# Causal mask of the softmax maxima: from a table added on VectorE to a bf16 product accumulated by TensorE

## The chip, the cores and the metric

The kernel runs on one core of a Trainium2 chip (trn2). The metric is the device time of one execution in microseconds (us), lower is better. Below, "before" is the kernel as it was and "after" the changed one.

## The reference, cut to what matters

The program computes four layers on x of shape (4, 1024, 128): an attention with a compressed key/value and rotary parts, a top-1 mixture of experts, a dilated attention, and a last mixture with gates. Only the first attention is touched:

```
q = concat(q_content, rope(q_rope))      # 16 heads, 8 + 32 per head
k = concat(k_content, rope(k_rope))
scores = einsum('bhqd,bhkd->bhqk', q, k) / sqrt(40)
scores = where(tril(ones(T, T)), scores, -inf)      # T = 1024
attn = softmax(scores, axis=-1)
out = einsum('bhqk,bhkd->bhqd', attn, v)
```

A softmax needs the maximum of each query's row over the keys up to itself. How this maximum comes about is what changes.

## The kernel before

**Units.** The 4 x 16 heads are worked as 32 units of two heads (`NU`). For each unit SyncE gathers queries and keys into the tiles `Qp` and `Kp` (four of each in rotation), with parts laid out so that one matmul over 120 rows gives the scores.

**Two passes.** A unit's scores are computed twice. The first pass (kind `mx`, L604) has queries on partitions and keys along the row: for query tile `qt` (0 to 7, each 128 queries) the keys 0 to 128(qt+1). VectorE takes the row maxima from it (L833 to L840). They are transposed (kind `mxT`, L608), negated (L847) and written by a DMA into row 120 of `Qp`. The second pass (kind `st`, L615) has keys on partitions; row 120 subtracts the maximum inside the product, ScalarE takes the exponential (L717), GpSimd zeroes what lies past the diagonal (L907), and TensorE multiplies by the values (kind `pv`, L632).

**Slots.** `S` is three PSUM tiles of 1024 columns, two banks of 512 each. Every `mx`, `st`, `rope`, `oT`, `mxT` and the like takes the next slot in rotation, and TensorE waits until what was in it has been drained. For the kinds of `BY_HALF` ("mx", "st", "rope") both the filling and the draining are signalled by half, with two steps of the semaphore for each item.

**The order** is written out beforehand in `Attn0.order`. Each of 12 steps of a unit issues one `st` and one `mx` (of a later unit, 12 + 3 steps ahead), every second step a `pv`; rotations of the next group of units and the next batch's preparation are strewn in between. All engines walk through the same list.

**The maxima.** An `mx` item is one query tile and one part of the keys: part 0 the first 512, part 1 the rest (for qt of 4 and more). Half h of the slot holds head h. A part 0 of a qt of 4 and more is a plain maximum into `first` (L833). Every other item ends on the diagonal: L836 adds the table `later` (zeros, then the 128x128 triangle `mqk` of 0 and -1e30) and takes the maximum in one fused instruction, followed by a read of the accumulator. After qt = 0 the two parts are merged (L840). That is 8 reduces, 16 fused instructions and one merge for each unit.

**Semaphores**: `made(kind)` counts what TensorE has filled, `done(kind)` what has been drained.

Of the kernel before, what the change touches and what calls it, by code (L numbers as in the profile page):

```python
# [7 lines left out]
F32R = mybir.dt.float32r  # L8
BF16 = mybir.dt.bfloat16
U32 = mybir.dt.uint32  # L10
ALU = mybir.AluOpType
ACT = mybir.ActivationFunctionType
AX = mybir.AxisListType
# [76 lines left out]
class Program:  # L90
# [44 lines left out]
    def sb(self, st, name, shape, dt=F32):  # L135
        return st.enter_context(self.nc.sbuf_tensor(name, shape, dt))
# [39 lines left out]

BY_HALF = ("mx", "st", "rope")


def free_half(p, lane, w, h):  # L180

    if w.before:
        kind, n = w.before
        lane.wait_ge(p.done(kind), 2 * n - 1 + h if kind in BY_HALF else n)
# [164 lines left out]
for n, (name, i) in enumerate((("cq", 0), ("cq", 1), ("ck", 0), ("ck", 1))):  # L349
    for later, kind in enumerate(("rope", "spin", "high", "low")):  # L350
        at = 8 + 4 * n + later
# [7 lines left out]
class Attn0:  # L359
    names = ("wkd", "wvd", "wo0")  # L360

    def __init__(self, p, st, route):
        self.route = route
        def sb(name, shape, dt=F32):
            return p.sb(st, name, shape, dt)
# [7 lines left out]
        self.cos, self.sin = within(p.low, 0, T), within(p.low, T, T)  # L373
        self.later = sb("later", [128, 512])
        self.xnT = within(p.mid, 0, T)
# [6 lines left out]
        self.P = [sb(f"P{i}", [128, 2, 512]) for i in range(NP0)]  # L382
        self.mx, self.first, self.mT = sb("mx", [128, 2, 8]), sb("first", [128, 2, 4]), sb("mT", [16, 128], F32R)
        self.oT, self.rec, self.osum = sb("oT", [128, 512]), sb("rec", [128, 4, 2]), sb("osum", [128, 4, 2, 9])
# [6 lines left out]
    def order(self, o):  # L391
        start = len(o.items)
# [9 lines left out]

        pieces = [(qt, part) for qt in range(7, -1, -1) for part in range(qt // 4 + 1)]

# [68 lines left out]
def shipped(p, lane, u, *names):  # L473

    for name in names:
        lane.wait_ge(p.sem(f"d_{name[1]}{u % 4}"), 128 * (u // 4 + 1))
# [21 lines left out]
def attn0_sync(p, k, f0, sp, ye):  # L498
    a = p.a
    x_in = a["x"].rearrange("(n p) d -> p n d", p=128)  # L500
    for i in range(2):
        ye.dma_start(p.x[:, 4 * i:4 * i + 4, :], x_in[:, 4 * i:4 * i + 4, :]).then_inc(p.sem("d_x").h, 16)
    for t, n in ((k.cos[:], "cos"), (k.sin[:], "sin"), (k.R["ck"][:], "wkr"), (k.later[:, 384:512], "mqk")):
        ye.dma_start(t, a[n]).then_inc(p.sem("d_c").h, 16)
# [35 lines left out]
CONSTS0, WEIGHTS0 = 16 * 4, 16 * 5  # L540


def attn0_tensor(p, k, pe, te):
    S, A, W = p.S, p.A, k.W
    for w in k.items:
        s = w.slot
# [12 lines left out]
        elif w.kind == "kv":  # L559
            pe.wait_ge(p.done("xnT"), w.n)  # L560
            pe.wait_ge(p.sem("d_w"), WEIGHTS0)
            for i in range(8):
                ins = te.matmul(S[s][:, 32 * i:32 * i + 32], k.xnT[:, 128 * i:128 * i + 128], k.wkv[:], start=True, stop=True)
# [4 lines left out]
        elif w.kind in ("cq", "ck"):  # L568
# [7 lines left out]
            for i in range(2):  # L576
                c = slice(512 * i, 512 * i + 512)
                ins = te.matmul(S[s][:, c], weight[:], src[:, c], start=True, stop=True)
# [18 lines left out]
        elif w.kind == "mx":  # L597
            u, qt, part = w.at
            Q, K, n = k.Q[u % 4], k.K[u % 4], min(512, 128 * (qt + 1) - 512 * part)
            pe.wait_ge(p.sem("g_ones"), 1)  # L600
            shipped(p, pe, u, "cq", "ck")
            for h in range(2):
                free_half(p, pe, w, h)
                te.matmul(S[s][:, 512 * h:512 * h + n], Q[0:120, h, 128 * qt:128 * qt + 128],  # L604
                          K[0:120, h, 512 * part:512 * part + n], start=True, stop=True).then_inc(p.made("mx").h, 1)
        elif w.kind == "mxT":
            pe.wait_ge(p.done("mx"), 24 * w.n)
            te.transpose(S[s][0:16, 0:128], k.mx[:].rearrange("p h n -> p (h n)"), p.ident[:]).then_inc(p.made("mxT").h, 1)  # L608
        elif w.kind == "st":
            u, qh, kb, c = w.at  # L610
# [122 lines left out]
def attn0_vector(p, k, f0, dve, ve):  # L733
    S, x = p.S, p.x
    ve.memset(k.later[:, 0:384], 0.0)
    for A in p.A:
        ve.memset(A[:], 0.0).then_inc(p.sem("v_zero").h, 1)
    for w in k.items:
        s = w.slot
# [21 lines left out]
        elif w.kind == "ln4":  # L761
            b = w.at[0]
            ln_apply(p, ve, k.xn, x[:, 8 * b:8 * b + 8, :], range(4, 8)).then_inc(p.sem("v_xn").h, 1)
            if b == 0:
                dve.wait_ge(p.sem("d_w"), WEIGHTS0)
                ve.tensor_scalar(k.W["wkd"][:], k.W["wkd"][:], k.gkv[:, 0:1], None, ALU.mult)
                ve.tensor_scalar(k.W["wvd"][:], k.W["wvd"][:], k.gkv[:, 0:1], None, ALU.mult).then_inc(p.sem("v_weights").h, 1)
# [57 lines left out]
        elif w.kind == "mx":  # L825
            u, qt, part = w.at
            if u:
                dve.wait_ge(p.made("mxT"), u)
            n = 128 * (qt + 1) - 512 * part
            for h in range(2):  # L830
                dve.wait_ge(p.made("mx"), 2 * w.n - 1 + h)
                if part == 0 and qt >= 4:
                    ve.tensor_reduce(k.first[:, h, qt - 4:qt - 3], S[s][:, 512 * h:512 * h + 512], AX.X, ALU.max).then_inc(p.done("mx").h, 1)  # L833
                    continue
                of = S[s][:, 512 * h:512 * h + n]
                ins = ve.tensor_tensor_reduce(out=of, in0=of, in1=k.later[:, 512 - n:512], scale=1.0, scalar=-3e38, op0=ALU.add, op1=ALU.max,  # L836
                                              accum_out=k.mx[:, h, qt:qt + 1])
                if qt == 0 and h == 1:
                    dve.then(ins)
                    ins = ve.tensor_tensor(k.mx[:, :, 4:8], k.mx[:, :, 4:8], k.first[:], ALU.max)  # L840
                ins.then_inc(p.done("mx").h, 1)
        elif w.kind == "mxT":
# [1648 lines left out]
```

## Time and profile before

| | |
|---|---|
| median of 3 runs | 1527.55 us (1525.64 to 1531.12) |
| profiled execution: span from its first to its last instruction | 1519.5 us |
| the runs' median above this span | 8.05 us |
| the first attention's units, from the first maxima to the last | 60 to 813 us of the span |
| TensorE busy in the span | 1254.7 us (83%) |
| VectorE busy in the span | 1153.3 us (76%) |

The profiled execution has no time of its own beside its span in the records. The 8.05 us are what lies around the span.

How to read the profile: PE is TensorE (PEld its weight loads), DVE VectorE, ACT ScalarE, POOL GpSimd, SP SyncE. "Busy" is the time covered by records of an engine. L604 is line 604 of the kernel. In `S<-Kp,Qp` the tile written stands ahead of the arrow and the tiles read behind it.

### The profile page before, as it was taken

Reading aid. Unit: us, or ns where it says so; the run is one execution under the profiler, and the core shown is the slowest. Engines: PE = TensorE matmul, PEld = TensorE weight load, DVE = VectorE, ACT = ScalarE, POOL = GpSimd, SP = SyncE. Lnnn points to the kernel's source line nnn. Section 1 sums busy time; section 2 is a strip of 40 time slices with the busy share of each in tenths; the row PEclk is TensorE's granted clock in tenths of the full one; section 3 lists DMA queues with packets and bytes.
Section 4 is the critical chain, followed back from the end, with each engine's and each line's share of the span. In section 5 each row is a group of like instructions: output and inputs, shape, how many; then the busy total and the mean of one; then the engine's idle time right before and its main releaser. Section 6 shows DMA issues by size and latency. Waiting matters only on the chain.

```text
span 1519.5 us, 38187 instructions
## 1 busy us (share of the span) xinstructions
PE 1254.7 (83%) x13524; PEld 854.0 (56%) x13524; DVE 1153.3 (76%) x3936; ACT 832.7 (55%) x2003; POOL 690.7 (45%) x1043
## 2 busy tenths in 40 slices
PE   5489899998899888999888899959988999557780
PEld 2344444445455454454444799947777778546660
DVE  5588787897898977989875755547799988755666
ACT  1145456554555544555556545438887767326663
POOL 3023232333233333324313454556687888674664
PEclk9689999998999989999999989977898877568995
DMA  4665726557266472573770221021111112222335
GB/s 112 102 104 83 117 36 94 90 84 117 32 89 113 62 120 36 84 127 47 122 221 28 83 59 37 22 65 45 45 46 47 54 51 75 94 73 79 89 87 172
DMA packets 73886, 123.25 MB, mean 81 GB/s; under 512 B 17534, under 2 KB 46083, under 8 KB 72800
## 3 DMA queue, kind: packets, MB, share of 16 engines
q1 hardware_dynamic: 63896, 104.97, 36.4%
q0 software_dynamic: 7616, 13.59, 2.8%
q10 hardware_dynamic: 2184, 2.25, 0.7%
q8 instruction: 108, 1.77, 0.5%
q14 instruction: 82, 0.67, 0.1%
HBM read 30.40 MB, written 17.60 MB: 32 GB/s over the span
## 4 chain that ended last, share of the span: by engine, by line
PE 39%; DVE 31%; issue 10%; POOL 8%; ACT 7%; DMA 4%; DVEq 1%; SPq 0%; ACTq 0%; POOLq 0%
DVE first L833 5%; PE A L632 5%; PE S L1099 5%; PE S L615 4%; PE S L604 4%; DVE S L836 4%; DMA Qp<-mT 2%; DVE tA L812 2%; POOL xq L1468 2%; PE A L1106 2%; PE S L1659 2%; DVE tB L813 2%; PE S L596 2%; PE S L194 2%; PE A L1670 2%
## 5 line engine op out<-in xcount | busy, mean ns | idle before, releaser
L717 ACT ACTIVATE P<-S 128x512 f32<-128x512 f32 (+3 forms) x768 | 333.4, 491 | 286.2 <-PE S L615 281.8
L907 POOL TENSOR_SCALAR_AFFINE_SELECT P<-P 128x256 f32<-128x256 f32 (+1 forms) x256 | 116.5, 459 | 390.2 <-ACT P L717 390.1
L615 PE MATMUL S<-Qp,Kp 121*128 121x512 f32 (+3 forms) x768 | 254.8, 396 | 35.1 <-DVE tB L813 9.6
L604 PE MATMUL S<-Kp,Qp 120*128 120x512 f32 (+3 forms) x768 | 255.0, 402 | 33.1 <-DMA Kp<-big 16.1
L836 DVE CUSTOM_DVE_ANT_0 S<-S,later 128x512 f32<-128x512 f32 (+3 forms) x512 | 239.0, 512 | 44.3 <-PE S L604 43.1
L604 PEld LDWEIGHTS S<-Kp,Qp 120*128 120x128 f32 x768 | 136.0, 199 | 168.0 <-issue 76.3
L615 PEld LDWEIGHTS S<-Qp,Kp 121*128 121x128 f32 x768 | 141.1, 195 | 111.4 <-issue 24.1
L833 DVE TENSOR_REDUCE first<-S 128x1 f32<-128x512 f32 x256 | 164.3, 683 | 48.8 <-PE S L604 48.6
L632 PE MATMUL A<-P,V 128*9 128x512 f32 (+3 forms) x1536 | 176.6, 508 | 5.1 <-POOL P L907 5.0
L2264 POOL DMA_INDIRECT yq<-yq,id x71 | 70.4, 991 | 51.5 <-DVE id L2221 23.2
L1896 POOL TENSOR_TENSOR prod<-mid,kT 128x128 f32<-128x128 f32 x160 | 68.2, 460 | 51.0 <-ACT mid L1727 34.4
L895 POOL TENSOR_TENSOR big<-tA,big 128x1024 fp32r<-128x1024 f32 x28 | 66.3, 2368 | 43.5 <-ACT big L679 43.5
L1767 ACT ACTIVATE low<-sc,mn 128x64 f32<-128x64 f32 x336 | 82.4, 336 | 4.8 <-DVE sc L1831 4.8
L1099 PE MATMUL S<-xgT,we 128*128 128x128 f32 x624 | 79.8, 283 | 2.9 <-ACT we L1122 2.2
L1099 PEld LDWEIGHTS S<-xgT,we 128*128 128x128 f32 x624 | 76.2, 199 | 3.5 <-issue 2.4
L1659 PE MATMUL S<-kT,Qm 32*32 32x64 f32 x4096 | 61.5, 231 | 19.1 <-issue 7.9
L1468 POOL DMA_INDIRECT xq<-n,posu x64 | 64.5, 1007 | 28.2 <-issue 13.6
L836 DVE DVE_READ_ACCUMULATOR2_ANT mx<- 128x1 f32 x512 | 71.1, 139 | 0.0
L1302 POOL DMA_INDIRECT ys<-yo,id x39 | 38.4, 986 | 64.9 <-DVE yo L1273 62.5
L1659 PEld LDWEIGHTS S<-kT,Qm 32*32 32x32 f32 x4096 | 48.2, 108 | 33.5 <-issue 19.8
L2110 PE MATMUL S<-xqT,wq 128*128 128x128 f32 x284 | 48.6, 295 | 19.3 <-DVE wq L2210 17.2
L2160 ACT ACTIVATE hq<-S,wq 128x128 f32<-128x128 f32 x142 | 44.3, 363 | 29.0 <-PE S L2110 26.1
(358 smaller groups left out, 2637.3 us busy)
## 6 DMA issues: line engine op xcount, KB each, us to landing
Qp<-big SPq DMA_DIRECT2D x63, 256.0 KB
Kp<-big SPq DMA_DIRECT2D x62, 256.0 KB
Qp<-big SPq DMA_DIRECT2D x63, 128.0 KB
Kp<-big SPq DMA_DIRECT2D x62, 128.0 KB
xq<-xq SPq DMA_DIRECT2D x71, 72.0 KB, 1.9
yb<-yq SPq DMA_DIRECT2D x8, 528.0 KB, 7.1
big<-in_w SPq DMA_DIRECT2D x4, 1024.0 KB, 9.6
big<-vt SPq DMA_DIRECT2D x32, 128.0 KB
```

The costliest lines, as they stand in the source:

```text
L604: te.matmul(S[s][:, 512 * h:512 * h + n], Q[0:120, h, 128 * qt:128 * qt + 128], K[0:120, h, 512 * part:512 * part + n], start=True, stop=T ...
L615: te.matmul(S[s][:, 512 * h + c:512 * h + 512], K[0:121, h, 128 * kb:128 * kb + 128], Q[0:121, h, 512 * qh + c:512 * qh + 512], start=True ...
L632: ins = te.matmul(A[oa][o:o + 9, c:512], k.V[u // 8 % 2][:, kb, 2 * (u % 8) + h, :], k.P[(e.n - 1) % NP0][:, h, c:512], start=kb < 2, stop ...
L717: se.activation(k.P[(w.n - 1) % NP0][:, h, c:512], S[s][:, 512 * h + c:512 * h + 512], ACT.Exp, scale=SCALE0).then_inc(p.done("st").h, 1)
L833: ve.tensor_reduce(k.first[:, h, qt - 4:qt - 3], S[s][:, 512 * h:512 * h + 512], AX.X, ALU.max).then_inc(p.done("mx").h, 1)
L836: ins = ve.tensor_tensor_reduce(out=of, in0=of, in1=k.later[:, 512 - n:512], scale=1.0, scalar=-3e38, op0=ALU.add, op1=ALU.max, accum_out= ...
L907: ge.affine_select(P[:, :, start:c + 128], P[:, :, start:c + 128], [[0, 2], [1, wide]], ALU.is_ge, 0.0, base=start - c, channel_multiplier ...
L1099: ins = te.matmul(S[s][:, c:c + 128], k.we[t % NW][:, c:c + 128], k.xgT[t % NH][:], start=True, stop=True)
L1468: ge.indirect_dma_start(r.xq, bass.IndirectOffsetOnAxis(r.posu[q][:, h, i:i + 1], 0), r.n2[q][h][:, i, :], None).then_inc(p.sem(f"d_xq{q}" ...
L1659: ins = te.matmul(C[32 * q:32 * q + 32, 64 * h:64 * h + 64], k.Qm[c % 2][rows, j, 128 * i + 32 * q:128 * i + 32 * q + 32], k.kT[c % 2][row ...
L1767: ins = se.activation(pr[:, h, :], k.sc[t % 2][:, h, 0:64], ACT.Exp, bias=k.mn[t % 2][:, h:h + 1])
L2264: ge.indirect_dma_start(k.yq, bass.IndirectOffsetOnAxis(k.id[t % 8][:, 0:1], 0), k.yo[t % NY1][:], None, bounds_check=2 * B * T - 1, oob_i ...
```

## The change

- The first attention gets three small tiles: `mqk` (the triangle in f32, as loaded), `mask` (the same in bf16) and `eye` (the identity in bf16). VectorE makes `eye` and `mask` once at the start. The table `later` and the tile `first` go.
- An `mx` item is now, for qt of 4 and more, one query tile and one head, with both banks of the slot for this head's keys; for the others it is one query tile with both heads, one for each bank.
- Behind the matmul that ends on the diagonal, TensorE adds eye^T x mask into the last 128 columns (L611 of after), as a second, accumulating product.
- `mx` leaves `BY_HALF`: TensorE signals once, behind the last mask, VectorE takes one plain maximum over the item (L842, L844 of after) and signals once. There are 12 such items a unit, as before.

```diff
-BY_HALF = ("mx", "st", "rope")
+BY_HALF = ("st", "rope")
...
-        pieces = [(qt, part) for qt in range(7, -1, -1) for part in range(qt // 4 + 1)]
+        pieces = [(qt, h) for qt in range(7, -1, -1) for h in range(qt // 4 + 1)]
...
         elif w.kind == "mx":
-            u, qt, part = w.at
-            Q, K, n = k.Q[u % 4], k.K[u % 4], min(512, 128 * (qt + 1) - 512 * part)
+            u, qt, head = w.at
+            Q, K, n = k.Q[u % 4], k.K[u % 4], 128 * (qt + 1)
             pe.wait_ge(p.sem("g_ones"), 1)
+            pe.wait_ge(p.sem("v_weights"), 1)
             shipped(p, pe, u, "cq", "ck")
-            for h in range(2):
-                free_half(p, pe, w, h)
-                te.matmul(S[s][:, 512 * h:512 * h + n], Q[0:120, h, 128 * qt:128 * qt + 128],
-                          K[0:120, h, 512 * part:512 * part + n], start=True, stop=True).then_inc(p.made("mx").h, 1)
+            for half in range(2):
+                h, lo = (head, 512 * half) if qt >= 4 else (half, 0)
+                many, last = min(512, n - lo), n - lo <= 512
+                free_half(p, pe, w, half)
+                te.matmul(S[s][:, 512 * half:512 * half + many], Q[0:120, h, 128 * qt:128 * qt + 128],
+                          K[0:120, h, lo:lo + many], start=True, stop=not last)
+                if last:
+                    at = 512 * half + many
+                    ins = te.matmul(S[s][:, at - 128:at], k.eye[:], k.mask[:], start=False, stop=True)
+            ins.then_inc(p.made("mx").h, 1)
         elif w.kind == "mxT":
-            pe.wait_ge(p.done("mx"), 24 * w.n)
+            pe.wait_ge(p.done("mx"), 12 * w.n)
...
             if b == 0:
+                dve.wait_ge(p.sem("d_c"), CONSTS0)
+                dve.wait_ge(p.sem("d_id"), 16)
+                ve.tensor_copy(k.eye[:], p.ident[:])
+                ve.tensor_copy(k.mask[:], k.mqk[:])
...
         elif w.kind == "mx":
-            u, qt, part = w.at
+            u, qt, head = w.at
             if u:
                 dve.wait_ge(p.made("mxT"), u)
-            n = 128 * (qt + 1) - 512 * part
-            for h in range(2):
-                dve.wait_ge(p.made("mx"), 2 * w.n - 1 + h)
-                if part == 0 and qt >= 4:
-                    ve.tensor_reduce(k.first[:, h, qt - 4:qt - 3], S[s][:, 512 * h:512 * h + 512], AX.X, ALU.max).then_inc(p.done("mx").h, 1)
-                    continue
-                of = S[s][:, 512 * h:512 * h + n]
-                ins = ve.tensor_tensor_reduce(out=of, in0=of, in1=k.later[:, 512 - n:512], scale=1.0, scalar=-3e38, op0=ALU.add, op1=ALU.max,
-                                              accum_out=k.mx[:, h, qt:qt + 1])
-                if qt == 0 and h == 1:
-                    dve.then(ins)
-                    ins = ve.tensor_tensor(k.mx[:, :, 4:8], k.mx[:, :, 4:8], k.first[:], ALU.max)
-                ins.then_inc(p.done("mx").h, 1)
+            n = 128 * (qt + 1)
+            dve.wait_ge(p.made("mx"), w.n)
+            if qt >= 4:
+                ins = ve.tensor_reduce(k.mx[:, head, qt:qt + 1], S[s][:, 0:n], AX.X, ALU.max)
+            else:
+                ins = ve.tensor_reduce(k.mx[:, :, qt], S[s][:].rearrange("p (h n) -> p h n", h=2)[:, :, 0:n], AX.X, ALU.max)
+            ins.then_inc(p.done("mx").h, 1)
```

The order of TensorE in a step that fills a slot for qt = 6 beside scores, before (the semaphore `rd_x` is `done` of kind x):

```order
L604 MATMUL S<-Kp,Qp 128x512 [waits rd_mx] x2
L615 MATMUL S<-Qp,Kp 128x512 [waits rd_rl,d_m1]
L615 MATMUL S<-Qp,Kp 128x512
L604 MATMUL S<-Kp,Qp 128x384 [waits rd_st] x2
L615 MATMUL S<-Qp,Kp 128x384 [waits rd_mx] x2
```

And the same kind of place in the changed kernel:

```order
L607 MATMUL S<-Kp,Qp 128x512 [waits rd_st]
L607 MATMUL S<-Kp,Qp 128x384
L611 MATMUL S<-mask,eye 128x128
L622 MATMUL S<-Qp,Kp 128x512 [waits rd_mx,d_m1]
L622 MATMUL S<-Qp,Kp 128x512
L607 MATMUL S<-Kp,Qp 128x512 [waits rd_st]
L607 MATMUL S<-Kp,Qp 128x384
L611 MATMUL S<-mask,eye 128x128
```

Both heads' first 512 keys were one item and their last 384 another, each half with a wait of its own ("x2" with a wait means one wait for each). Now each head is an item of 512 + 384 with one wait ahead and a mask behind.

VectorE in the first unit, before (ISA is the fused add-and-maximum and its accumulator read):

```order
L833 TENSOR_REDUCE first<-S 128x1 [waits pe_mx] x2
L836 ISA S,mx<-S,later 128x128 [waits pe_mx]
L836 ISA mx 128x1
L836 ISA S,mx<-S,later 128x128 [waits pe_mx]
L836 ISA mx 128x1
...
L840 TENSOR_TENSOR mx<-mx,first 128x2x4 [waits own_dve]
L847 TENSOR_SCALAR mT<-S 16x128 [waits pe_mxT]
```

And in the changed kernel, the whole unit:

```order
L842 TENSOR_REDUCE mx<-S 128x1 [waits pe_mx] x8
L844 TENSOR_REDUCE mx<-S 128x2 [waits pe_mx] x4
L851 TENSOR_SCALAR mT<-S 16x128 [waits pe_mxT]
```

Twelve reduces, each with one wait, stand where 8 reduces, 16 fused instructions with their reads and a merge had stood.

## Rows read from the trace of the kernel before

**Rows 1.** The page, its first part: span, busy time of each engine
```profile
span 1519.5 us, 38187 instructions
PE 1254.7 (83%) x13524; PEld 854.0 (56%) x13524; DVE 1153.3 (76%) x3936; ACT 832.7 (55%) x2003; POOL 690.7 (45%) x1043
```

**Rows 2.** Busy time by stretches: the stretch, its us, then each engine; clock, DMA
```profile
60.00:813.00 753.00, 675.12 (x3707) 363.06 (x3707) 621.53 (x2169) 400.34 (x863) 232.44 (x352) 0.96 0.57 93
```

**Rows 3.** The chain of waits from 60 to 813 us, shares by line
```profile
by line: issue 11.1%; DVE first L833 11.1%; PE A L632 9.9%; PE S L615 8.7%; PE S L604 8.1%; DVE S L836 7.8%; DMA Qp<-mT 4.9%; DVE tA L812 4.8%; DVE tB L813 3.9%; POOL big L895 2.8%; PE S L596 2.6%; ACT P L717 2.1%; DVE tA L818 2.0%; DVE tA 
```

**Rows 4.** Waits from 60 to 813 us: who for whom, us, times, longest
```profile
PEld S L615 <- DVE first L833: 21.7, 56, 0.5
PEld S L604 <- DVE first L833: 19.4, 41, 2.2
PEld S L604 <- DVE mx L836: 19.1, 38, 0.9
PEld S L615 <- DVE mx L836: 15.6, 47, 0.6
...
DVE first L833 <- PE S L604: 48.6, 53, 12.5
DVE S L836 <- PE S L604: 43.1, 43, 3.2
```

**Rows 5.** VectorE's groups by form: busy us, mean ns of one; idle before
```profile
L833 DVE TENSOR_REDUCE first<-S 128x1 f32<-128x512 f32 x256 | 164.3, 683 | 48.8 <-PE S L604 48.6
L836 DVE CUSTOM_DVE_ANT_0 S<-S,later 128x512 f32<-128x512 f32 x128 | 85.7, 710 | 24.8 <-PE S L604 24.8
L836 DVE DVE_READ_ACCUMULATOR2_ANT mx<- 128x1 f32 x512 | 71.1, 139 | 0.0
L1829 DVE TENSOR_REDUCE mx<-sc 128x16 f32<-128x1104 f32 x32 | 41.7, 1303 | 3.3
```

**Rows 6.** Timeline of VectorE in the first unit: start us, us, what
```profile
64.51 1.29 DVE L833 TENSOR_REDUCE first<-S 128x1 f32<-128x512 f32 x2 [12.50 <-PE S L604]
...
66.97 1.28 DVE L833 TENSOR_REDUCE first<-S 128x1 f32<-128x512 f32 x2
68.17 0.56 DVE L836 CUSTOM_DVE_ANT_0 S<-S,later 128x384 f32<-128x384 f32 x1
...
76.50 0.17 DVE L840 TENSOR_TENSOR mx<-mx,first 128x8 f32<-128x8 f32 x1
```

**Rows 7.** Timeline of TensorE at 445 to 453 us
```profile
445.61 0.95 PE L261 MATMUL S<-rw,aT 128*128 128x8 f32 x8
446.42 0.70 PE L615 MATMUL S<-Qp,Kp 121*128 121x512 f32 x2
446.96 0.51 PE L604 MATMUL S<-Kp,Qp 120*128 120x384 f32 x2
447.31 0.52 PE L615 MATMUL S<-Qp,Kp 121*128 121x384 f32 x2
...
452.98 0.24 PE L269 MATMUL S<-hot,one 128*128 128x8 bf16 x4
453.08 0.70 PE L615 MATMUL S<-Qp,Kp 121*128 121x512 f32 x2
```

**Rows 8.** Timeline, then chain of waits, at 455 to 458 us
```profile
455.50 0.73 PE L604 MATMUL S<-Kp,Qp 120*128 120x512 f32 x2
456.03 0.70 DVE L836 CUSTOM_DVE_ANT_0 S<-S,later 128x512 f32<-128x512 f32 x1 [0.32 <-PE S L604]
...
456.94 1.00 PE L604 MATMUL S<-Kp,Qp 120*128 120x384 f32 x2
...
455.57 0.44 PE S L604
...
456.03 0.27 DVE S L836
...
457.49 0.44 PE S L604
```

**Rows 9.** TensorE's groups by form: the nearest whole 128x128 product of 128 columns
```profile
L1099 PE MATMUL S<-xgT,we 128*128 128x128 f32 x624 | 79.8, 283 | 2.9 <-ACT we L1122 2.2 <-DVE hh L1267 0.7
```

More of the change, by code:

```diff
@@ L373, in __init__ @@
         self.cos, self.sin = within(p.low, 0, T), within(p.low, T, T)
-        self.later = sb("later", [128, 512])
+        self.mqk, self.mask, self.eye = sb("mqk", [128, 128]), sb("mask", [128, 128], BF16), sb("eye", [128, 128], BF16)
         self.xnT = within(p.mid, 0, T)
@@ L382, in __init__ @@
         self.P = [sb(f"P{i}", [128, 2, 512]) for i in range(NP0)]
-        self.mx, self.first, self.mT = sb("mx", [128, 2, 8]), sb("first", [128, 2, 4]), sb("mT", [16, 128], F32R)
+        self.mx, self.mT = sb("mx", [128, 2, 8]), sb("mT", [16, 128], F32R)
         self.oT, self.rec, self.osum = sb("oT", [128, 512]), sb("rec", [128, 4, 2]), sb("osum", [128, 4, 2, 9])
@@ L502, in attn0_sync @@
         ye.dma_start(p.x[:, 4 * i:4 * i + 4, :], x_in[:, 4 * i:4 * i + 4, :]).then_inc(p.sem("d_x").h, 16)
-    for t, n in ((k.cos[:], "cos"), (k.sin[:], "sin"), (k.R["ck"][:], "wkr"), (k.later[:, 384:512], "mqk")):
+    for t, n in ((k.cos[:], "cos"), (k.sin[:], "sin"), (k.R["ck"][:], "wkr"), (k.mqk[:], "mqk")):
         ye.dma_start(t, a[n]).then_inc(p.sem("d_c").h, 16)
@@ L734, in attn0_vector @@
     S, x = p.S, p.x
-    ve.memset(k.later[:, 0:384], 0.0)
     for A in p.A:
```

## The prediction

> **What bounds the kernel now.** I read the page first: over the whole span of 1519.5 us TensorE is busy 83% and VectorE 76% [rows 1]. That is an average over several layers, so I cut out the stage of the first attention with the view by stretches. Between 60 and 813 us (753 us, all 32 units) TensorE is busy 675 us and VectorE 622 us, at a mean granted clock of 0.96 [rows 2]. Neither number says that its engine is full. A TensorE record holds the tail of its matmul (the next one starts long before it ends), and VectorE has 131 us idle.
>
> The chain of waits of this stretch is mixed [rows 3]: the two maxima lines of VectorE hold 11.1 + 7.8 = 18.9% of it, 142 us, and the matmuls that fill slots for the maxima (L604) hold 8.1%, 61 us; scores (L615) and values (L632) have 18.6% more. So the work passes to and fro between the two engines through the three score slots. The view of waits shows it from both sides [rows 4]: VectorE sat idle 53 + 43 = 96 times, 92 us in all (12.5 us of them one wait at the start, for Kp), because the slot of a maximum was not yet filled; and TensorE's next weight load, for scores or for maxima, stood 56 + 41 + 38 + 47 = 182 times, 76 us, because VectorE had not yet emptied a slot. Each engine waits for the other: this is a loop with latency, not one full engine. The reader is to see that a change that takes work from VectorE, but makes each hand-over coarser, acts on both sides.
>
> **What VectorE saves.** Per unit it does 8 reduces of 512, 16 fused add-and-maximum instructions over 128 to 512, each with its accumulator read, and one merge. In the first unit nothing else is on the engine: from 64.51 to 76.67 us, 12.16 us [rows 6]. After the change the same 9216 elements go through 12 plain reduces. One of 512 takes 683 ns and one of 1104 takes 1303 ns [rows 5], so 620/592 = 1.047 ns an element; two of 512 follow each other every 0.60 us (66.97 to 68.17) [rows 6], so what one adds beside its elements is 0.60 - 0.536 = 0.064 us. That gives 9216 x 1.047 + 12 x 64 ns = 10.4 us a unit. The saving is 1.76 us a unit, 56 us over 32 units. (The records would promise more, 710 + 139 ns against 683 ns for 512 elements [rows 5], but records overlap; the starts are what counts.) The rate for a view across two banks of a slot, or of two heads at once, is not in the trace. I take the same rate.
>
> Only what lies on the chain shortens the end. 142 us of about 12.16 x 32 = 389 us of this work are on it, 0.37. So **-21 us** (bounds: 0 if the loop hides it, -56 if VectorE decides everywhere).
>
> **What TensorE adds.** Sixteen mask products a unit, 512 in all, each a weight load of eye and 128 bf16 columns. No such product is in the trace; the nearest rows bound it. Columns: two matmuls of 384 columns follow within 0.35 us (446.96 to 447.31), 0.46 ns a column, so 128 of them are 0.059 us. Its own bf16 weights cost almost nothing where something streams before: four bf16 products with 128x128 weights and 8 columns take 452.98 to 453.08, 0.025 us each. But the next f32 weight load takes 0.10 us where little covers it (eight of them with 8 columns each, 445.61 to 446.42), and behind a mask it has only 0.06 us of cover instead of the 0.17 to 0.23 us of a wide matmul [rows 7]. So 0.06 us at the least, 0.28 us at the most (the mean of one whole 128x128 f32 record [rows 9]), and I take 0.11 us, because load and stream are limited by the slower of the two here. That is 56 us of TensorE time. Of the 768 fills of L604 about three in ten (222) are on the chain, counted along its steps, so **+17 us**.
>
> The Trainium skill (TensorE: Matmul & The Clock Gate, Back-to-back issue gap) gives about 81 ns for one pair of load and matmul with 128 columns. By that the term would be 12 us instead of 17, an estimate. No row here has such a pair.
>
> **What the hand-over loses.** Before, a slot went over by halves: VectorE starts when head 0 is filled, and TensorE may refill half 0 while VectorE empties half 1. Now VectorE waits for both banks and the masks, and frees the slot once. "mx" also leaves the list of kinds that wait by half, so its first fill waits for the whole slot.
>
> Toward VectorE: at 455.50 TensorE starts two fills of 512, and VectorE, idle for 0.32 us, starts at 456.03 behind the first of them [rows 8]. Now it has to wait for the second fill (0.18 us for the mean 384 columns) and its mask (0.11 us). Such a step, from L604 straight to a maximum, is on the chain 52 times (one is 455.57 to 456.03) [rows 8]: 52 x 0.29 = **+15 us**. Behind it on VectorE stand the output sums and the rotations, which move with it.
>
> Toward TensorE: at 457.49 the chain goes from the maximum of half 1 back to L604 for half 1 alone [rows 8]; half 0 had been filled from 456.94 on. Now both fills come behind the freeing: 49 such steps on the chain x 0.18 = **+9 us**. Where the other parity decides, half a drain (0.5 us) could come on top at some steps; I leave that to the range. For a fill of maxima over a slot of scores the wait for the whole slot costs nothing: that ACT is done early enough, and the waits of [rows 4] that name VectorE are the ones that bind.
>
> The Trainium skill has a rule that speaks against the change (Perfetto Trace Analysis, Optimizing Scalar/DVE Operations): grouping into larger operations pays if the engine is saturated, and where it is not but leaves bubbles on others, breaking instructions up lets work finish sooner. The rows put this stage in the second case: 83% busy, with waits on both sides. By the first half of that rule the time would come out as in rival A.
>
> **Edits that cost nothing.** The two copies to bf16 at the start stand behind xnT's last operand, before a stretch in which VectorE waits for TensorE. The memset of the table (384 columns) goes. Moving mqk's DMA target changes no transfer. The first unit is included in the sum. No queue gets another DMA.
>
> **Sum.** -21 + 17 + 15 + 9 = +20 us. The span goes from 1519.5 to about 1539.5 us; the median of the runs, 1527.55 us, lies 8.05 us above that span, and with the same difference I forecast **1547.5 us**. About 0.3% (5 us) is what a measurement of this kernel can tell from no change.
>
> **Rivals.**
>
> A. *VectorE is what decides, and the masks run in TensorE's gaps.* For it: TensorE's 76 us of waits for the maxima [rows 4], into which the 56 us of masks could fall, and the 12.16 us that shrink to 10.4. Against it: the 96 times in which VectorE itself was idle for want of a filled slot. Half of the full 56 us would then be won: about 1500 us. It decides if VectorE's backlog lasts through most steps. Chance 0.27. This is also what the skill's rule of grouping on a saturated engine would give (Perfetto Trace Analysis).
>
> B. *The terms cancel.* If a mask costs 0.06 us (term 9 instead of 17) and half of the hand-overs find slack, the sum is -21 + 9 + 8 + 4 = 0: 1527.5 us. Chance 0.13.
>
> C. *The masks are dear.* If the accumulating bf16 product can't overlap with its f32r neighbours, each costs 0.28 us: 143 us, of which three in ten are 43 us, and the sum is +46 us. With half a drain at the 9 places where half 0 alone had been waited for, +50: 1578 us. It decides from 0.2 us a mask. Chance 0.12.
>
> That the change doesn't do what it says is no case here: in the order VectorE has 12 reduces a unit and TensorE 16 masks.
>
> **How the numbers follow.** The forecast, a loss of 5 to 35 us around +20, has 0.48, and A 0.27, B 0.13, C 0.12. The range goes from 1500, which cuts the better half of A off, to 1576, which leaves out most of C: about 2 in 10 outside. Faster by over 0.3%: A and a small part of B, 0.29. Same: 0.13. Slower: the forecast, C and the rest, 0.58.
>
> **What would show it.** Right: the twelve reduces at 0.33 to 1.13 us from start to start, 10.4 us for the first unit; VectorE's busy time in the stage down by about 50 us; VectorE's idle time before maxima up from 92 us; TensorE's waits for maxima not below 76 us in spite of the faster drains; a mask at 0.11 us from start to start. Wrong: if the waits of TensorE for maxima nearly vanish and the stage gets shorter than 753 us, the saving was on the path far more than 0.37 and A holds; if a mask takes more than 0.2 us, C holds.

## The result, and the profile after

Before 1526.6 us, the change 1561.41 us (medians of 4 runs each), ratio 1.0217 with a 95% interval of 1.0175 to 1.0259. The change was timed a second time, in the last group of experiments: 1548.93 us against 1525.46 us, ratio 1.0154 [1.0116, 1.0192]. It is slower in both, by 23 to 35 us.

The table of the section before puts 8.05 us down to what lies around the span. The later records show otherwise: where a run is listed with its time and its span, the two differ by 1.7 to 1.9 us. So the profiled execution of the kernel before took about 1521.3 us (an estimate: its span and 1.8 us) and was 6 us faster than its median, while the profiled execution of the change, 1566.61 us, was the slowest of its four (1552.16 to 1566.61). Spans alone therefore overstate the loss by about 10 us.

The parts of the page and of the stretches that answer to [rows 1] and [rows 2], for the changed kernel:

```profile
span 1564.9 us, 38284 instructions
PE 1307.4 (84%) x14036; PEld 885.4 (57%) x14036; DVE 1102.0 (70%) x3009; ACT 833.5 (53%) x2003; POOL 688.5 (44%) x1043
...
60.00:836.00 776.00, 702.72 (x4220) 371.44 (x4221) 574.95 (x1242) 399.71 (x863) 229.94 (x352) 0.98 0.55 91
```

VectorE lost 51 us of busy time and 927 instructions over the span, as the change means it to, and the span still grew by 45 us (the medians by 35). Where it grew is seen from the last exponential of the first attention, the group of the exponentials by line, before and after (shortest, median and longest in ns; start of the first and of the last in us):

```profile
L717 ACT ACTIVATE P<-S x768: 257/543/659, 82.5 to 829.7; 128x512 f32<-128x512 f32 x128, 128x256 f32<-128x256 f32 x64
```
```profile
L724 ACT ACTIVATE P<-S x768: 258/542/653, 81.7 to 852.2; 128x512 f32<-128x512 f32 x128, 128x256 f32<-128x256 f32 x64
```

The stage ends 22.5 us later. The other half of the 45 us lies behind it, and 20 us of it in the third layer: from the first to the last of its 4096 score matmuls it takes 273.8 us before, 294.2 us in the change's first profile and 276.3 us in its second (shortest, median and longest in ns; first and last start in us):

```profile
L1659 PE MATMUL S<-kT,Qm x4096: 210/214/312, 1014.5 to 1288.3; 32*32 32x64 f32 x196
```
```profile
L1663 PE MATMUL S<-kT,Qm x4096: 211/236/312, 1037.8 to 1332.0; 32*32 32x64 f32 x196
```
```profile
L1663 PE MATMUL S<-kT,Qm x4096: 211/214/312, 1039.8 to 1316.1; 32*32 32x64 f32 x196
```

In the profiles of the other eleven kernels it takes 274 to 284 us. Stretches of 266 us from that layer, of before, of the change (22 us later), and of its second profile:

```profile
1002.00:1268.00 266.00, 238.53 (x6586) 191.35 (x6590) 221.56 (x596) 207.35 (x619) 198.15 (x323) 0.83 0.19 54
```
```profile
1024.00:1290.00 266.00, 243.20 (x6087) 197.30 (x6088) 204.19 (x560) 191.65 (x572) 181.19 (x295) 0.71 0.17 48
```
```profile
1024.00:1290.00 266.00, 237.33 (x6498) 189.57 (x6498) 220.89 (x601) 203.33 (x604) 194.09 (x317) 0.81 0.18 51
```

The first profile of the change has a mean granted clock of 0.71 there and gets 8% fewer matmuls through (6087 for 6586); the second has 0.81 and nearly the number of before. The code of that layer is the same in all three. So the loss of the stage, 22 to 24 us, is the change's. The 12 us more of the first comparison came with a lower clock in a layer that the change does not touch. The medians move with the clock in the same way when nothing is changed: of the 17 runs of before in the last group, the two slowest (1532.73 and 1532.81 us) have a mean granted clock of 0.888, the two fastest (1518.18 and 1518.54 us) 0.905 and 0.907. Differences of a few us between medians are to be read with that, and the end of the stage beside them.

The waits of the stage (60 to 836 us) answer to [rows 4]:

```profile
PEld S L607 <- DVE mx L842: 26.2, 47, 2.4
PEld S L622 <- DVE mx L842: 22.4, 51, 0.9
PEld S L607 <- DVE mx L844: 14.9, 28, 0.7
...
PEld S L622 <- DVE mx L844: 1.2, 7, 0.2
...
DVE mx L842 <- PE S L611: 94.1, 114, 13.1
DVE mx L844 <- PE S L611: 57.4, 49, 2.8
```

VectorE now sits idle 163 times, 151 us, for a slot of maxima to be filled, where it had been 96 times and 92 us. TensorE's weight loads, for scores and for maxima, wait 65 us instead of 76. The engine that got less work waits more for it, and the other one gains little.

The first unit answers to [rows 6]; its twelve reduces stand in two rows of VectorE's timeline:

```profile
64.91 7.54 DVE L842 TENSOR_REDUCE mx<-S 128x1 f32<-128x1024 f32 x8 [13.09 <-PE S L611]
72.37 3.00 DVE L844 TENSOR_REDUCE mx<-S 128x2 f32<-128x1024 f32 x4
```

From 64.91 to 75.37 us, 10.46 us, against 12.16 before.

### The profile page after: what moved, and what is told of

The parts are those of the page before. It is cut to its first block, busy times and chain, and to the rows that moved or that the text cites. A ratio compares the mean times of both kernels' runs of the same rounds, so it can differ in the third digit from the quotient of the medians.

```text
span 1564.9 us, 38284 instructions
## 1 busy us (share of the span) xinstructions
PE 1307.4 (84%) x14036; PEld 885.4 (57%) x14036; DVE 1102.0 (70%) x3009; ACT 833.5 (53%) x2003; POOL 688.5 (44%) x1043
## 4 chain that ended last, share of the span: by engine, by line
PE 51%; DVE 22%; POOL 8%; ACT 7%; issue 5%; DMA 2%; DVEq 1%; ACTq 1%; SPq 0%; POOLq 0%
PE S L607 8%; PE A L639 7%; PE S L622 6%; DVE mx L842 5%; PE S L1103 4%; PE S L1663 3%; DVE tA L822 2%; POOL xq L1472 2%; PE A L1674 2%; DVE mx L844 2%; PE A L1110 2%; PE S L194 2%; DVE tB L823 2%; PE S L611 2%; POOL big L899 2%
## 5 line engine op out<-in xcount | busy, mean ns | idle before, releaser
L842 DVE TENSOR_REDUCE mx<-S 128x1 f32<-128x1024 f32 (+3 forms) x256 | 257.0, 1020 | 95.5 <-PE S L611 94.1
L622 PE MATMUL S<-Qp,Kp 121*128 121x512 f32 (+3 forms) x768 | 250.0, 405 | 33.4 <-DVE mx L842 19.6
L607 PE MATMUL S<-Kp,Qp 120*128 120x512 f32 (+3 forms) x768 | 245.7, 395 | 37.9 <-DMA Kp<-big 17.1
L622 PEld LDWEIGHTS S<-Qp,Kp 121*128 121x128 f32 x768 | 123.7, 196 | 68.0 <-issue 25.6
L844 DVE TENSOR_REDUCE mx<-S 128x2 f32<-128x1024 f32 (+3 forms) x128 | 104.9, 823 | 60.4 <-PE S L611 57.4
L611 PE MATMUL S<-mask,eye 128*128 128x128 bf16 x512 | 118.4, 234 | 0.0
L611 PEld LDWEIGHTS S<-mask,eye 128*128 128x128 bf16 x512 | 50.5, 99 | 71.6 <-issue 52.2
L1663 PE MATMUL S<-kT,Qm 32*32 32x64 f32 x4096 | 65.1, 250 | 16.7 <-ACT Qm L1738 9.6
```

The lines of the kernel that those rows point to most:

```text
L607: te.matmul(S[s][:, 512 * half:512 * half + many], Q[0:120, h, 128 * qt:128 * qt + 128], K[0:120, h, lo:lo + many], start=True, stop=not last)
L611: ins = te.matmul(S[s][:, at - 128:at], k.eye[:], k.mask[:], start=False, stop=True)
L622: te.matmul(S[s][:, 512 * h + c:512 * h + 512], K[0:121, h, 128 * kb:128 * kb + 128], Q[0:121, h, 512 * qh + c:512 * qh + 512], start=True ...
L842: ins = ve.tensor_reduce(k.mx[:, head, qt:qt + 1], S[s][:, 0:n], AX.X, ALU.max)
L844: ins = ve.tensor_reduce(k.mx[:, :, qt], S[s][:].rearrange("p (h n) -> p h n", h=2)[:, :, 0:n], AX.X, ALU.max)
L1663: ins = te.matmul(C[32 * q:32 * q + 32, 64 * h:64 * h + 64], k.Qm[c % 2][rows, j, 128 * i + 32 * q:128 * i + 32 * q + 32], k.kT[c % 2][row ...
```

## The experiments

Three groups of four kernels, each timed beside the kernel before. Medians of before: 1526.55 us for the first four kernels below, 1527.86 us for the next four and 1525.46 us for the last four. Below each is given with its ratio to before and with the end of the first attention, the start of the last exponential (829.7 us before, 852.2 after). That end is read from one profiled execution each, the ratio from all runs.

### The whole hand-over alone

```diff
-BY_HALF = ("mx", "st", "rope")
+BY_HALF = ("st", "rope")
...
-                te.matmul(S[s][:, 512 * h:512 * h + n], Q[0:120, h, 128 * qt:128 * qt + 128],
-                          K[0:120, h, 512 * part:512 * part + n], start=True, stop=True).then_inc(p.made("mx").h, 1)
+                ins = te.matmul(S[s][:, 512 * h:512 * h + n], Q[0:120, h, 128 * qt:128 * qt + 128],
+                                K[0:120, h, 512 * part:512 * part + n], start=True, stop=True)
+            ins.then_inc(p.made("mx").h, 1)
...
+            dve.wait_ge(p.made("mx"), w.n)
             for h in range(2):
-                dve.wait_ge(p.made("mx"), 2 * w.n - 1 + h)
...
-                ins.then_inc(p.done("mx").h, 1)
+            ins.then_inc(p.done("mx").h, 1)
```

> The kernel before with one part of the change alone: a slot of maxima goes over whole (one signal behind both fills, one behind both drains), table, fused instructions and items as before, no mask on TensorE. Theory H (the loss is the coarser hand-over plus the masks on a chain that both engines share): later starts on VectorE 52 x 0.18 = 9 us and fills behind the whole drain 49 x 0.18 = 9 us, so +18 us, 1545 us, and the first stage ends near 831 us instead of 813. Rival M (the masks alone cost the time): no change, 1527 us. Rival C (the loss sits in the later layers' lower clock and not in this stage): the stage ends at 813 us.

1569.09 us, ratio 1.0291 [1.0257, 1.0326]: +44 us. The group of the exponentials:

```profile
L718 ACT ACTIVATE P<-S x768: 257/543/662, 82.5 to 872.9; 128x512 f32<-128x512 f32 x128, 128x256 f32<-128x256 f32 x64
```

43 us later, nearly all of the loss. With table, fused instructions and items as before and no mask, the coarser hand-over alone costs more than the whole change. Its waits from 60 to 880 us, against [rows 4]:

```profile
PEld S L616 <- DVE first L834: 44.5, 54, 1.1
PEld S L604 <- DVE first L834: 32.4, 42, 2.8
PEld S L604 <- DVE mx L837: 30.4, 44, 1.2
PEld S L616 <- DVE mx L837: 18.2, 28, 1.0
...
DVE first L834 <- PE S L604: 73.1, 84, 12.7
DVE S L837 <- PE S L604: 57.6, 57, 3.0
```

TensorE's waits go from 76 to 126 us and VectorE's from 92 to 131 us, with the same work on both engines. The loss is paid on both sides. Along the chain of waits to the last exponential, a fill for maxima (L604) is followed straight by a maximum 101 times here, where the same count gives 46 for the kernel before (the pieces called "issue" left out; the prediction's own count was 52).

### The change without the masks

```diff
-                te.matmul(S[s][:, 512 * half:512 * half + many], Q[0:120, h, 128 * qt:128 * qt + 128],
-                          K[0:120, h, lo:lo + many], start=True, stop=not last)
-                if last:
-                    at = 512 * half + many
-                    ins = te.matmul(S[s][:, at - 128:at], k.eye[:], k.mask[:], start=False, stop=True)
+                ins = te.matmul(S[s][:, 512 * half:512 * half + many], Q[0:120, h, 128 * qt:128 * qt + 128],
+                          K[0:120, h, lo:lo + many], start=True, stop=True)
```

> The changed kernel without the mask products: the maxima run over the keys past the diagonal too, within the last tile (the causal mask is left out of the maxima alone; the exponentials are still masked). Theory H: against the changed kernel's 1561 us the masks' 17 us on the chain and their part in the later starts, 6 us, go: 1538 us, still 11 us above the kernel before. Rival M: the hand-over costs nothing and VectorE's saving stays, 1527 - 21 = 1506 us. Rival C: as slow as the changed kernel, about 1560 us, if its clock is as low.

1532.18 us, ratio 1.0032 [1.0009, 1.0056]. The stage ends where it ended before:

```profile
L721 ACT ACTIVATE P<-S x768: 258/542/653, 79.5 to 830.1; 128x512 f32<-128x512 f32 x128, 128x256 f32<-128x256 f32 x64
```

From the run above to this one, 1569 to 1532 us, VectorE's plain maxima, one instruction for each item and the change of the items give back 37 us (43 us of the stage); this step does not tell them apart. From this one to the change the masks cost 22 us of the stage, and 1.2% (second timing) to 1.9% (first) of the whole. Both rivals of the expectation are out: with a free hand-over this kernel would have come to 1506 us, and with the loss in the later layers' clock it would have stayed at about 1560 us. The hand-over is not free, and the masks are not all.

### The mask products in the kernel before

```diff
+            pe.wait_ge(p.sem("v_weights"), 1)
             for h in range(2):
                 free_half(p, pe, w, h)
+                edge = part == 1 or qt < 4
...
+                if edge:
+                    ins = te.matmul(S[s][:, 512 * h + n - 128:512 * h + n], k.eye[:], k.eye[:], start=False, stop=True)
+                ins.then_inc(p.made("mx").h, 1)
```

> The kernel before, by half and with its table, plus 512 bf16 products with the same shape as the masks (the identity is added to the last tile, which raises a few maxima by up to 1 and leaves the softmax as it is). It prices the products alone. Theory H: 17 us on the chain and 6 us in VectorE's later starts, 1550 us. Rival M: about 55 us, since the change as a whole lost 34 us in spite of the 21 us that VectorE saves: 1582 us. If the products hide in TensorE's gaps: 1527 us.

1535.56 us, ratio 1.0059 [1.0028, 1.0091], the stage ends at 837.2 us (+7.5):

```profile
L723 ACT ACTIVATE P<-S x768: 258/541/656, 79.4 to 837.2; 128x512 f32<-128x512 f32 x128, 128x256 f32<-128x256 f32 x64
```

Expected were 23 us. The same 512 products cost 9 us here, by half beside the fused instruction, and 22 us of the stage in the change. So their price is not a property of the product alone. That the hand-over by itself makes the difference is not shown: between the two the maxima and the items differ as well (see "No masks, by half" below).

### Masks and plain maxima, by half

The run above with the real mask (the tiles and the copies of the change, without the table), and in place of the fused instruction:

```diff
-                ins = ve.tensor_tensor_reduce(out=of, in0=of, in1=k.later[:, 512 - n:512], scale=1.0, scalar=-3e38, op0=ALU.add, op1=ALU.max,
-                                              accum_out=k.mx[:, h, qt:qt + 1])
+                ins = ve.tensor_reduce(k.mx[:, h, qt:qt + 1], of, AX.X, ALU.max)
```

> The mask products and plain maxima of the change, but items and hand-over by half as before (8 + 16 reduces and one merge for each unit, no fused instruction). VectorE's work is 9216 x 1.047 ns + 24 x 64 ns + 0.37 us = 11.6 us a unit instead of 12.16, 18 us over all units, 7 us of them on the chain. Theory H: -7 + 23 = +16 us, 1543 us. Rival M: -7 + 55 = +48 us, 1575 us.

1530.51 us, ratio 1.0029 [1.0001, 1.0058], stage to 833.8 us. Against the run above it is 5 us less (3 us of the stage), where -7 was expected for VectorE's 18 us of saved work. The whole comes out at +4 us where +16 was expected.

### No masks, by half

The kernel before with the same replacement of the fused instruction and nothing else.

> The kernel before, by half as before, with plain maxima instead of the fused instruction and no mask anywhere in the maxima (the causal mask is left out of the maxima alone). Masks by half cost 9 us in all (the run with extra products) and the plain maxima by half gave back 5: so -5 us, 1522 us, if the two prices add up. If VectorE were the limit when nothing else is in the way, its 18 us of saved work would show: 1509 us.

1517.38 us, ratio 0.9934 [0.991, 0.9958]: 10 us faster than before, the fastest of all. The stage ends at 818.0 us, 12 us earlier:

```profile
L717 ACT ACTIVATE P<-S x768: 258/542/656, 81.6 to 818.0; 128x512 f32<-128x512 f32 x128, 128x256 f32<-128x256 f32 x64
```

Twice the 5 us expected: VectorE's saved work, forecast at 18 us, gives 10 to 12 us where no mask stands between the engines, and 3 to 5 us where one does. Read the other way, from this run to the one above it, the masks cost 13 us of the median (15 us by the ratios) and 16 us of the stage (818.0 to 833.8 us), by half and with plain maxima. So 9 us was their price only beside the slower fused instruction, and against the 22 us of the stage in the change the hand-over and the items together leave a difference of 6 us. The prices of the parts do not add up; each holds beside what else is in the kernel. This kernel leaves out the causal mask of the maxima, which may then be larger than the largest allowed score; the softmax is the same as long as the difference stays small enough for the exponentials.

### The three parts of the hand-over, one by one

Each of these is the kernel before with one edit.

Filled whole, drained by half:

```diff
-                dve.wait_ge(p.made("mx"), 2 * w.n - 1 + h)
+                dve.wait_ge(p.made("mx"), 2 * w.n)
```

> The kernel before, but VectorE starts a slot of maxima only when both halves are filled; it still frees them one by one. One of the three parts of the whole hand-over, which together cost 44 us in all and 43 us in the first stage. Theory H as predicted: 9 us of 18, scaled to the 43 measured: about 21 us, 1548 us. Rival (all of the loss is on TensorE's side, since VectorE has a backlog in most steps): no change, 1527 us.

1551.82 us, ratio 1.0166 [1.0136, 1.0196], +24 us; the stage ends at 856.2 us (+26.5).

Filled by half, drained whole:

```diff
-        lane.wait_ge(p.done(kind), 2 * n - 1 + h if kind in BY_HALF else n)
+        lane.wait_ge(p.done(kind), 2 * n if kind == "mx" else 2 * n - 1 + h if kind in BY_HALF else n)
```

> The kernel before, but whoever refills a slot of maxima waits for both of its drains; VectorE still starts at the first filled half. Theory H scaled: about 21 us, 1548 us. Rival (TensorE's side holds all of it): 43 us, 1570 us. If the starts of VectorE hold all of it: 1527 us.

1542.56 us, ratio 1.0107 [1.0076, 1.0137], +15 us; the stage ends at 835.7 us (+6). The median lost more than the stage of the profiled execution did, but that execution was the fastest of its six (1531.72 to 1545.41 us).

Only the first fill of maxima waits for its whole predecessor:

```diff
-        if w.kind not in BY_HALF:
+        if w.kind not in BY_HALF or w.kind == "mx":
             free_slot(p, pe, w)
```

> The kernel before, but the first fill of a slot of maxima waits for the whole slot of its predecessor (an effect of taking the kind out of the list, which the prediction put at nothing). As predicted: no change, 1527 us. Rival: where the predecessor is itself a slot of maxima (a third of the cases) this is the same wait as in the run with whole drains, so up to a third of that loss, 7 to 14 us.

1535.48 us, ratio 1.0069 [1.004, 1.0099], +8 us; the stage ends at 832.0 us (+2). Here too the profiled execution was the fastest, of ten (1525.89 to 1544.49 us).

The medians give 24 + 15 + 8 = 47 us against 44 us for all three at once, the stages 26.5 + 6 + 2 = 35 us against 43. The near agreement of the medians is no proof that the parts add up, because the last two overlap: in the order, 136 of the 384 items of maxima take a slot that held maxima before, and their first fill waits for both drains in either run. By both readings the largest part is VectorE's later start. Its waits and TensorE's, 60 to 880 us, in the run filled whole:

```profile
DVE first L833 <- PE S L604: 69.3, 84, 13.1
DVE S L836 <- PE S L604: 54.6, 47, 4.3
...
PEld S L615 <- DVE first L833: 38.7, 95, 1.0
PEld S L604 <- DVE mx L836: 27.2, 64, 1.6
PEld S L604 <- DVE first L833: 25.8, 64, 2.2
PEld S L615 <- DVE mx L836: 16.6, 49, 0.6
```

One wait was moved, on VectorE, and TensorE's four rows went from 182 times and 76 us to 272 times and 108 us. The delay comes back round the ring of slots, and the chain of waits now has 88 places where a fill is followed straight by a maximum, for 46 before.

### The change once more

No edit.

> The changed kernel itself once more, beside the runs below. The first stage should end near 852 us again (before: 830). If the further 12 us of its median belong to the change, the rest of the kernel is slower than before in this run too (1561 us); if they came from the granted clock that the later layers happened to get, the median comes down towards 1527 + 23 = 1550 us.

1548.93 us, ratio 1.0154 [1.0116, 1.0192]; the stage ends at 853.5 us, as in the first profile. The median came down to what the stage alone explains (about 1550 us).

### The masks twice

```diff
+                    te.matmul(S[s][:, at - 128:at], k.eye[:], k.mask[:], start=False, stop=False)
                     ins = te.matmul(S[s][:, at - 128:at], k.eye[:], k.mask[:], start=False, stop=True)
```

> The changed kernel with every mask product issued twice (the second adds another -1e30 past the diagonal and changes no maximum). The products cost 22 us of the first stage where the slot goes over whole and 8 us where it goes over by half. Theory (each product lies between TensorE and VectorE in the loop, so it is paid at most steps): the second one has its weights' load covered by the first and costs its 59 ns of columns and the start of VectorE: +12 to +20 us on the changed kernel. Rival (TensorE has gaps enough): no more than 5 us.

1566.94 us, ratio 1.0285 [1.0242, 1.0328]: 18 us more than the change of the same group; the stage ends at 867.8 us, 14 to 16 us later. 512 more products for 14 to 18 us are 0.03 us each, about half of the 0.059 us of their columns. The expectation (+12 to +20 us) holds.

### The change without the first fill's wait

```diff
-        if w.kind not in BY_HALF:
+        if w.kind not in BY_HALF and w.kind != "mx":
             free_slot(p, pe, w)
```

> The changed kernel, but the first fill of maxima waits only for half 0 of a predecessor that is freed by half (scores, rotations). The run with this wait alone added 2 us to the first stage of the kernel before and 8 us to its median. Theory: 2 to 8 us less than the changed kernel. If the wait is covered: no change against it.

1550.68 us, ratio 1.0159 [1.0119, 1.0199], stage to 851.8 us: no change against the 1548.93 us of the same group. In the changed kernel this wait is covered. It concerns slots of scores and rotations alone; the run in the kernel before also held back the fills over maxima, so the two do not contradict each other.

### One head for each item, masks, by half

The run "Masks and plain maxima, by half" with the items of the change:

```diff
-        pieces = [(qt, part) for qt in range(7, -1, -1) for part in range(qt // 4 + 1)]
+        pieces = [(qt, head) for qt in range(7, -1, -1) for head in range(qt // 4 + 1)]
...
+            for half in range(2):
+                dve.wait_ge(p.made("mx"), 2 * w.n - 1 + half)
+                h, part = (head, half) if qt >= 4 else (half, 0)
```

> Masks on TensorE, plain maxima and the hand-over by half, with the items of the change (both banks of one head). Against the run with masks by half (1530.5 us) only the items' sizes are evened out: 512 + 128 to 512 + 512 instead of 1024 and 256 to 1024 in turn. Theory (the hand-over is what decided, the items do not matter): within 5 us of 1530 us. Rival (the even items are part of what the change gained where it goes over whole): 1515 us or less.

1520.83 us, ratio 0.9974 [0.9948, 1.0001]. It lies between the expectation (within 5 us of 1530 us) and its rival (1515 us or less): 10 us below the run with the items of before (1530.51 us; 8 us by the ratios, as the two were timed in different groups), and its stage ends 12 us earlier, 8 us earlier than before:

```profile
L724 ACT ACTIVATE P<-S x768: 258/542/656, 82.0 to 821.8; 128x512 f32<-128x512 f32 x128, 128x256 f32<-128x256 f32 x64
```

The waits for the maxima nearly vanish on TensorE's side (60 to 880 us):

```profile
PEld S L608 <- DVE mx L847: 9.8, 13, 1.7
PEld S L622 <- DVE mx L847: 7.9, 27, 0.4
PEld S L608 <- DVE first L844: 6.7, 8, 2.2
...
PEld S L622 <- DVE first L844: 2.9, 5, 0.6
```

27 us where 76 had been, with the masks in. It is the fastest version with the exact mask; its interval just touches no change, so it is not shown to be faster than before. With the masks out it was not tried.

## Why the prediction was right, and where its sizes were not

The forecast was 1547.5 us, slower, and the change came out at 1561.4 and 1548.9 us. The mechanism was right in its direction: the two engines wait for each other, and the coarser hand-over and the masks cost more than VectorE's saved work gives. The size of the sum was luck. The profiled stage lost 22.5 us where the sum had +20, because two of its terms, the gain and the loss by the hand-over, were too small by amounts that cancel nearly. The sizes below hold for the order in which the parts were put in; in another order they come out otherwise.

**VectorE's work.** The first unit takes 10.46 us (10.4 forecast) and VectorE's busy time in the stage fell by 47 us (about 50). The rate across two banks is that of one (below). The share of it on the chain was mis-sized: -21 us was the term. In the whole hand-over the step from table and items of before to plain maxima and items of the change is worth -37 us. By half, a saving forecast at 18 us gave 10 to 12 us without masks and 3 to 5 us with them. The share is not the 0.37 of one chain; it moves with what else lies in the loop. The prediction did not price the evened items. By half and with masks they are worth 8 to 12 us; how much of the 37 us is theirs no run shows.

**The masks.** Forecast +17 us and their part of the later starts, 6 us, together 23; measured 22 us of the stage. This term came out, in this order of the steps; by half the same products cost 7.5 to 16 us of the stage. The price on TensorE itself, forecast at 0.11 us, can be read from this stretch of the changed kernel's timeline:

```profile
459.02 0.60 PE L607 MATMUL S<-Kp,Qp 120*128 120x512 f32 x2
459.47 0.23 PE L611 MATMUL S<-mask,eye 128*128 128x128 bf16 x1
459.51 0.60 PE L622 MATMUL S<-Qp,Kp 121*128 121x384 f32 x2
460.04 0.61 PE L639 MATMUL A<-P,V 128*9 128x256 f32 x8
```

The next scores start 0.04 us behind the mask (459.47 to 459.51). From the first of these two score matmuls of 384 columns to the group of values behind them it is 0.53 us (459.51 to 460.04). The same pair in the kernel before took 0.45 us, from 447.31 [rows 7] to the next row of its timeline:

```profile
447.76 0.61 PE L632 MATMUL A<-P,V 128*9 128x256 f32 x8
```

So a mask costs 0.04 us and 0.08 us more between the two scores behind it, 0.12 us together. It is so over the whole trace: where two scores of 256 columns follow a fill for maxima, the median from one start to the next is 0.12 us before and 0.20 us behind a mask (59 places each), and for 512 columns 0.24 and 0.31 us. That fits the weight load of the second score matmul, which the prediction saw left with too little cover; that the load is the reason was argued and not isolated.

**The hand-over.** This is the term that failed in size: 9 + 9 = +18 us without masks was forecast, and the whole hand-over alone costs 44 us. The later start of VectorE costs 24 us (forecast 9), the whole drain 15 us (forecast 9), and the wait of the first fill, which I had put at nothing, 8 us in the kernel before; in the changed kernel the part of it over scores and rotations does cost nothing. What failed behind the size is the count of steps. The prediction multiplied a delay by the steps that stood on the chain of the kernel before (52 and 49), as if the chain stayed where it was. Delaying the steps off the chain brings them onto it: a fill followed straight by a maximum is on it 46 times before, 88 times when VectorE starts later and 101 times with the whole hand-over, and the moved wait on VectorE gave TensorE 90 more waits.

**What would show it.** VectorE's idle time before maxima rose from 92 to 151 us, as forecast. TensorE's waits for maxima should not have fallen below 76 us and fell to 65. The experiments show where: they are 126 us with the whole hand-over alone, 87 us with plain maxima and even items on top (the run without masks), and 65 us with the masks, which take up TensorE's time where it had waited. A mask was to take 0.11 us and takes 0.12. Rival A fails: the change is slower, and VectorE was idle for 151 us before maxima. Rival B fails: a mask costs 0.12 us and not 0.06, and the terms cancel only in the run without masks (1532 us, the stage unchanged). Rival C fails: it needed 0.2 us a mask. Its own sum also left the mask in VectorE's later starts at 0.11 us; with 0.28 us they would be 24 us and not 15, and the sum +55 us.

The 8.05 us that the forecast adds to the span are no cost around it, as said above. The forecast is not moved by this: it amounts to the median of before plus the 20 us of the sum.

The rule of the Trainium skill that spoke against the change says that breaking instructions up may let work finish sooner where the engine is not saturated but leaves bubbles on others (Perfetto Trace Analysis, Optimizing Scalar/DVE Operations). The trace agrees in direction: VectorE is 83% busy with waits on both sides, and the change that groups its maxima is slower in both timings. The runs put the loss on the signals, though: with every instruction as before, the coarser hand-over alone cost 44 us. What the grouping of the instructions is worth by itself no run shows.

**What stays open.** Whether the lower clock of the third layer in the change's first profile (0.71 against 0.81 and 0.83) has to do with the change. The second timing did not show it, nor did the profiles of the other kernels (274 to 284 us for that layer), and no run was made for it. Open is also why the masks cost 22 us of the stage in the change, 16 us by half with plain maxima and 7.5 us by half with the fused instruction: the runs show the three prices and not their reason.

## What to carry to other kernels

Where two engines pass work through a small ring of buffers and each is seen waiting for the other, price a change by the hand-over first: what the consumer may start on and what the producer may refill. Here a signal by half instead of whole was worth 44 us, more than the 37 us that plain maxima and even items gave back. One instruction over both halves can wait and signal only for both, so a merge is to be weighed against the signal that it costs. Do not price a delay by the steps that are on the chain now; it brings others onto it. And try even sizes of the items, which here brought 8 to 12 us at equal work.

## What was unexpected of the hardware

A plain maximum over 1024 elements in two banks of PSUM takes 1219 ns, and 768 take 952 ns (the groups by form of the changed kernel), 1.04 ns an element, the rate that the prediction took from other rows (1.047 ns); a view of two heads at once is no dearer (1223 ns):

```profile
L842 DVE TENSOR_REDUCE mx<-S 128x1 f32<-128x1024 f32 x64 | 76.7, 1219 | 32.1 <-PE S L611 32.1
L842 DVE TENSOR_REDUCE mx<-S 128x1 f32<-128x768 f32 x64 | 60.9, 952 | 10.9 <-PE S L611 10.5
L844 DVE TENSOR_REDUCE mx<-S 128x2 f32<-128x1024 f32 x32 | 39.1, 1223 | 29.2 <-PE S L611 29.2
```

And the same program got a mean granted clock of 0.71 in one profiled execution and 0.81 in another over the same 266 us of its third layer, and that layer took 18 us longer (294.2 against 276.3 us), which accounts for the 16 us between their spans.
